# Values of a gated delta-rule layer: the four-tap convolution is moved from TensorE to VectorE

## The chip, the cores and the metric

The kernel runs on one core of one Trainium2 chip. The metric is the device time of one execution in microseconds (us). TensorE is called PE in the profile, VectorE DVE, ScalarE ACT, GpSimd POOL, and SyncE, which issues the transfers, SP.

## What is computed

The input is 8 sequences of 256 tokens with 128 channels. A feed-forward block, an attention-like block and an output projection follow one another. The change touches the first lines of the attention block:

```python
def _dwconv(x, w):                    # causal, each channel by itself, K taps
    ...
q = silu(_dwconv(hs @ Wq, conv_q))    # K = 4
k = silu(_dwconv(hs @ Wk, conv_k))
v = silu(_dwconv(hs @ Wv, conv_v))
beta = sigmoid(hs @ Wb)
o_d, _ = _delta_rule_chunkwise(bh(q), bh(k), bh(v), beta)   # chunks of 32 tokens
paths = [_dwconv(v, fir_s), _dwconv(v, fir_m), _dwconv(v, fir_l), o_d, v]
...
```

Here `hs` is the layer-normalised stream. `q` and `k` are scaled to unit length per head before the delta rule.

## The kernel before, in words

**Tiles.** The 2048 tokens are four tiles of 512 (two sequences each), with the channels on the partitions. The table `STEPS` lists steps `(kind, part, i)`, and every engine walks through that list in its order and does its own share of each step, so the list is the order of work on each engine. Part 0 is the first feed-forward, part 2 the attention, part 1 a last feed-forward. Semaphore counts come from the same list.

**Folded taps.** A convolution behind a projection is done by TensorE alone: `projections()` on VectorE multiplies a projection matrix by each tap (`taps`, one row per tap), which gives four matrices per projection in `conv_w` (12 for q, k and v, and one for beta). Each is kept as a rounded part and a rest, and so is the normalised input `xnp`; a product is three matmuls (high by high, high by low, low by high). So the step `qkv` of a tile issues 12 matmuls of 128x512 for each of q, k and v, on input shifted by one to four tokens, and 3 for beta: 39 in all (L825).

**Rings.** PSUM is eight banks: a ring `ps_a` of four that ScalarE empties (count `act_a`) and a ring `ps_d` of four that VectorE frees (count `dve_d`). `take_a(n)` and `take_d(n)` let TensorE write the n-th bank use only once use n-4 has been freed. Uses are counted in the order of `STEPS`.

**The stage around the change**, for tile t of the first two: `qkv` (t), `mean` (t+2), two `window` steps, `var` (t+2), `sumsq` (t). The steps `mean` and `var` are the layer norm of a later tile: TensorE centres (L792), ScalarE squares (L543), TensorE averages (L796), ScalarE takes a reciprocal root and squares it (L546, L549), VectorE refines the root and writes `xnp` (L985, L986, L991, L1102, L1104). The step `sumsq` sums the squares of q and k (TensorE L767), takes the root (ScalarE L621, L623) and normalises (VectorE L1155 to L1168). In `qkv` ScalarE applies Silu to q and k (L613), to the values (L608, into `vpad`), Tanh for beta (L611), and squares q and k (L616). `window` transposes pieces of `vpad` (TensorE L843, ScalarE L627). For tiles 2 and 3 there is no `mean` or `var`; the matmuls of `sumsq` 2 stand inside `qkv` 3, behind its first 12. Then `gram` 0 (TensorE L856, ScalarE L581, VectorE L1174), `lmat` (VectorE L1179), and a triangular solve on VectorE (L1069, L1072) that ends in the transposes before `yy` (L882).

## Time and profile before

| | us |
|---|---|
| median of 3 runs (lowest, highest) | 438.95 (436.8, 439.98) |
| profiled execution, its own time | 437.51 |
| its span in the trace | 435.7 |
| busy: TensorE, VectorE, ScalarE, GpSimd | 368.8, 294.9, 277.6, 42.0 |

The span is what the trace covers from the first to the last instruction; the own time is 1.8 us longer than it. Busy times overlap each other, so they don't add up to the span. The chain that ended last gives 60% of the span to TensorE, 24% to VectorE, 6% to ScalarE and 7% to stretches in which an engine waited for nothing that the profile shows ("issue").

### The profile page before, as it was taken

What the parts mean: (1) busy time and instruction counts of PE and PEld (TensorE: products, weight loads), DVE (VectorE), ACT (ScalarE), POOL (GpSimd) and SP (SyncE); (2) the same over time, 40 slices, a digit from 0 to 9 for tenths busy, and PEclk for the clock granted to TensorE, in tenths of its full rate; (3) what the DMA queues carried; (4) which work ended last, traced back from release to release, by engine and by line L of the source; (5) the groups of instructions that cost most, each with busy time, mean ns of one, the idle gap of its engine ahead of it and who ended that gap; (6) DMA issues with size and microseconds to landing.
All of it is one profiled execution on the core that took longest, in us unless ns stands there. A gap on an engine that the chain in (4) does not pass through costs nothing.

```text
span 435.7 us, 9783 instructions
## 1 busy us (share of the span) xinstructions
PE 368.8 (85%) x4132; PEld 277.2 (64%) x4132; DVE 294.9 (68%) x461; ACT 277.6 (64%) x434; POOL 42.0 (10%) x103
## 2 busy tenths in 40 slices
PE   5499999999999998799588489566599687978996
PEld 3377786678867776698477375433267464556885
DVE  1896579638307764789777968867858696478433
ACT  4788966879777786474243264515675948558963
POOL 5000000000000101000688600000000000000000
PEclk9799999999999998979955889686899898989999
DMA  7900007400000000070800000800000000001001
GB/s 267 341 3 1 3 1 214 128 2 2 1 2 0 0 2 3 3 210 16 217 5 5 2 5 2 264 5 2 0 2 3 1 2 1 2 2 50 2 2 48
DMA packets 14325, 19.75 MB, mean 45 GB/s; under 512 B 960, under 2 KB 9152, under 8 KB 14272
## 3 DMA queue, kind: packets, MB, share of 16 engines
q1 hardware_dynamic: 14128, 18.94, 14.6%
q8 instruction: 44, 0.72, 0.7%
q14 instruction: 9, 0.07, 0.1%
q10 hardware_dynamic: 144, 0.01, 0.0%
HBM read 17.91 MB, written 1.05 MB: 43 GB/s over the span
## 4 chain that ended last, share of the span: by engine, by line
PE 60%; DVE 24%; issue 7%; ACT 6%; DMA 2%; SPq 0%; DVEq 0%; ACTq 0%
PE ps_a L721 12%; PE ps_a L722 11%; PE ps_a L825 8%; PE ps_d L721 3%; PE ps_d L722 3%; PE ps_a L892 2%; PE ps_a L882 2%; DVE arena L1072 2%; DVE arena L1069 2%; PE ps_d L892 2%; PE ps_d L856 2%; PE ps_a L915 2%; DMA w_in<-in_h 2%; DVE hbuf L1114 2%; PE ps_a L913 2%
## 5 line engine op out<-in xcount | busy, mean ns | idle before, releaser
L721 PE MATMUL ps_a<-acts,w_f 128*128 128x512 f32 x256 | 103.7, 405 | 8.6 <-ACT acts L595 8.5
L722 PE MATMUL ps_a<-acts,w_f 128*128 128x512 f32 x256 | 101.6, 397 | 0.0
L721 PEld LDWEIGHTS ps_a<-acts,w_f 128*128 128x128 f32 x256 | 49.3, 192 | 22.0 <-ACT acts L595 10.2
L722 PEld LDWEIGHTS ps_a<-acts,w_f 128*128 128x128 f32 x256 | 49.2, 192 | 10.8 <-issue 0.7
L595 ACT ACTIVATE acts<-ps_a,vec 128x512 fp32r<-128x512 f32 x64 | 44.6, 697 | 0.0
L825 PE MATMUL ps_a<-xnp,conv_w 128*128 128x512 f32 x156 | 38.5, 404 | 0.0
L1138 DVE TENSOR_TENSOR acts<-gbuf,acts 128x512 fp32r<-128x512 f32 x32 | 21.6, 689 | 24.9 <-ACT acts L595 24.9
L1138 DVE TENSOR_TENSOR acts<-ghbuf,acts 128x512 fp32r<-128x512 f32 x32 | 21.2, 690 | 20.8 <-ACT acts L595 20.8
L825 PEld LDWEIGHTS ps_a<-xnp,conv_w 128*128 128x128 f32 x156 | 29.3, 188 | 8.2 <-issue 1.4
L985 DVE SCALAR_TENSOR_TENSOR arena<-ps_d,arena 128x512 f32<-128x512 f32 x16 | 11.0, 687 | 30.4 <-ACT arena L549 26.3
L592 ACT ACTIVATE gbuf<-ps_a,vec 128x512 f32<-128x512 f32 x32 | 22.3, 697 | 10.3 <-PE ps_a L722 10.1
L592 ACT ACTIVATE ghbuf<-ps_a,vec 128x512 f32<-128x512 f32 x32 | 22.4, 699 | 7.2 <-PE ps_a L722 7.1
L870 PE MATMUL ps_a<-toep,arena 96*32 96x96 f32 x512 | 23.7, 356 | 0.0
L721 PE MATMUL ps_a<-xn,w_f 128*128 128x512 f32 x32 | 15.3, 479 | 7.9 <-DVE ln L986 5.5
L870 PEld LDWEIGHTS ps_a<-toep,arena 96*32 96x32 f32 x512 | 19.3, 130 | 3.5 <-issue 1.3
L457 POOL TENSOR_TENSOR arena<-arena 128x31 f32<-128x31 f32 (+15 forms) x31 | 15.7, 505 | 46.7 <-DVE arena L1194 44.3
L904 PE MATMUL ps_d<-arena 32*32 32x64 f32 x448 | 11.7, 256 | 10.0 <-DVE arena L1222 6.6
L904 PEld LDWEIGHTS ps_d<-arena 32*32 32x32 f32 x448 | 9.0, 129 | 15.7 <-DVE arena L1222 8.3
L882 PE MATMUL ps_a<-arena 32*32 32x64 f32 x512 | 10.4, 242 | 10.1 <-DVE arena L1194 5.8
L640 ACT ACTIVATE arena<-ps_a 128x384 f32<-128x384 f32 x16 | 7.8, 490 | 16.7 <-PE ps_a L870 16.7
L1114 DVE SCALAR_TENSOR_TENSOR hbuf<-ps_d,vec,gbuf 128x512 f32<-128x512 f32 x16 | 11.6, 748 | 8.4 <-ACT gbuf L565 5.1
L459 POOL TENSOR_TENSOR arena<-arena 128x31 f32<-128x31 f32 (+15 forms) x31 | 16.7, 540 | 2.4
(211 smaller groups left out, 768.5 us busy)
## 6 DMA issues: line engine op xcount, KB each, us to landing
toep<-in_fir SPq DMA_DIRECT2D x24, 288.0 KB, 6.3
w_in<-in_h SPq DMA_DIRECT2D x4, 1024.0 KB, 8.6
g_rows<-in_gW SPq DMA_DIRECT2D x4, 640.0 KB, 6.6
w_in<-in_w SPq DMA_DIRECT2D x6, 256.0 KB, 4.4
iobuf<-in_x SPq DMA_DIRECT2D x4, 256.0 KB, 6.8
toep<-in_taps SPq DMA_DIRECT2D x1, 768.0 KB, 6.0
y<-iobuf SPq DMA_DIRECT2D x3, 256.0 KB, 2.3
toep<-in_proj SPq DMA_DIRECT2D x1, 256.0 KB, 8.6
```

The costliest lines, as they stand in the source:

```text
L459: own(e.tensor_tensor(sub, sub, prod, ALU.subtract))
L592: e.activation(gbuf[f][:, gi % 4], src[:, :], ACT.Gelu, scale=sc).then_inc(S["act_step"], 1)
L595: e.activation(acts[f][:, j % 3, 0, m], src[:, :], ACT.Gelu, scale=sc).then_inc(S["act_a"], 1)
L721: e.matmul(bank, w, hi, start=start, stop=False)
L722: return e.matmul(bank, w, lo, start=False, stop=stop)
L825: last = e.matmul(bank, conv_w[:, hw, ww], xnp[:, hx, 2 * i:2 * i + 2, o:o + L], start=n == 0, stop=n == len(todo) - 1)
L870: last = e.matmul(bank[32 * h:32 * h + 32, WIN * c4:WIN * c4 + WIN], vt[half][0:WIN, DH * h + 8 * grp + dl, :], toep[0:WIN, grp % 2, h, :, ...
L882: last = e.matmul(bank[r, 64 * n:64 * n + 64], xt[r, g, h, n], vk[r, g, h, n].rearrange("p x c -> p (x c)"), start=True, stop=True)
L892: last = e.matmul(bank[c, 64 * n:64 * n + 64], yu[r, g, h, n, o:o + DH], alt[g][r, h, n, 1:3].rearrange("p x c -> p (x c)"), start=True, s ...
L904: last = e.matmul(bank[r, 64 * b:64 * b + 64].rearrange("p (x t) -> p x t", x=2), s_sb[r, g, b], aqs[g][r, b, n], start=True, stop=True)
L1114: e.scalar_tensor_tensor(out=hbuf[f][:, m % 2], in0=ps_d[:, (dd + m) % NRING], scalar=vc("s2", m), in1=gbuf[f][:, (KT * j + m) % 4], op0=A ...
L1138: e.tensor_tensor(acts[f][:, j % 3, 1, m], gbuf[f][:, (KT * j + m) % 4], acts[f][:, j % 3, 0, m].bitcast(F32), ALU.subtract).then_inc(S["d ...
```

## The change

The values leave the step `qkv`. A new step `vproj` multiplies the normalised input by the unfolded `Wv`: three matmuls into one bank of the ring `ps_d`. VectorE then convolves from that bank into a buffer `vacc` (two of them, one per parity of the tile): one multiplication by the last tap, then three multiply-adds on shifted columns, each waiting for the one before. ScalarE's Silu reads `vacc` instead of PSUM, at the head of its share of `qkv`, and counts in `act_v`. `vproj` of tile 0 stands ahead of everything in the attention part, `vproj` of tile t+1 behind `qkv` of tile t. The folded weights shrink from 13 to 10 matrices; the four value taps reach `vec` by a second small transfer on ScalarE's queue.

```diff
-    s = []
+    s = [("vproj", 2, 0)]
     for t in range(2):
-        s += [("qkv", 2, t), ("mean", 2, t + 2), ("window", 2, 2 * t), ("window", 2, 2 * t + 1),
+        s += [("qkv", 2, t), ("vproj", 2, t + 1), ("mean", 2, t + 2), ("window", 2, 2 * t), ("window", 2, 2 * t + 1),
               ("var", 2, t + 2), ("sumsq", 2, t)]
-    s += [("qkv", 2, 2), ("window", 2, 4), ("window", 2, 5), ("sumsq", 2, 2), ("qkv", 2, 3), ("gram", 2, 0), ("lmat", 2, 0),
+    s += [("qkv", 2, 2), ("vproj", 2, 3), ("window", 2, 4), ("window", 2, 5), ("sumsq", 2, 2), ("qkv", 2, 3), ("gram", 2, 0), ("lmat", 2, 0),
...
-            e.dma_start(vec[:, 0:NVEC], d["vec"]).then_inc(S["ld_vec"], 16)
+            e.dma_start(vec[:, 0:NVEC], d["vec"][:, 0:NVEC]).then_inc(S["ld_vec"], 16)
+            e.dma_start(vc("vtap", 0, TAPS), d["vec"][:, NVEC:NVEC + TAPS]).then_inc(S["ld_vec"], 16)
...
-                    for w in range(4):
+                    e.wait_ge(S["dve_d"], D_AT[("vproj", 2, i)] + 1)
+                    e.activation(vpad[:, 2 * i:2 * i + 2, HIST:HIST + L], vacc[k2], ACT.Silu).then_inc(S["act_v"], 1)
+                    for w in range(3):
...
+                elif kind == "vproj":
+                    e.wait_ge(S["dve_xn"], VAR_AT[("var", 2, i)] + 1)
+                    bank = take_d(dd).rearrange("p (b t) -> p b t", b=2)
+                    for n, (hw, hx) in enumerate(((0, 0), (0, 1), (1, 0))):
+                        last = e.matmul(bank, conv_w[:, hw, 2 * TAPS], xnp[:, hx, 2 * i:2 * i + 2, PAD:PAD + L],
+                                        start=n == 0, stop=n == 2)
+                    last.then_inc(S["pe_d"], 1)
...
-                for w in range(3):
+                for w in range(2):
                     own(e.tensor_tensor(conv_s[:, TAPS * w:TAPS * w + TAPS],
...
-                own(e.tensor_copy(conv_s[:, 12], proj[:, 3]))
+                own(e.tensor_copy(conv_s[:, 2 * TAPS:NW], proj[:, 2:4]))
...
+                elif kind == "vproj":
+
+                    acc, z = vacc[i % 2], ps_d[:, dd % NRING].rearrange("p (b t) -> p b t", b=2)
+                    e.wait_ge(S["pe_d"], dd + 1)
+                    if i >= 2:
+                        e.wait_ge(S["act_v"], i - 1)
+                    own(e.tensor_scalar(acc, z, vc("vtap", TAPS - 1), None, ALU.mult))
+                    for back in range(1, TAPS):
+                        settle()
+                        tap = e.scalar_tensor_tensor(out=acc[:, :, back:L], in0=z[:, :, 0:L - back], scalar=vc("vtap", TAPS - 1 - back),
+                                                     in1=acc[:, :, back:L], op0=ALU.mult, op1=ALU.add)
+                        if back < TAPS - 1:
+                            own(tap)
+                        else:
+                            tap.then_inc(S["dve_d"], 1)
```

**TensorE around `sumsq` 1.** The rows show the last parts of `qkv` 1, the layer norm of tile 3, two windows (`ident,arena`), and `sumsq` 1 (`head_w`). Before:

```order
L825 MATMUL ps_a1<-xnp,conv_w 128x512 [waits act_a]
L825 MATMUL ps_a1<-xnp,conv_w 128x512 x11
L825 MATMUL ps_a2<-xnp,conv_w 128x512 [waits act_a]
L825 MATMUL ps_a2<-xnp,conv_w 128x512 x2
L792 MATMUL ps_d<-x_t,cent_w 128x512 [waits dve_d]
L843 MATMUL ps_a3<-ident,arena 96x128 [waits act_a]
L843 MATMUL ps_a3<-ident,arena 96x128 x3
L843 MATMUL ps_a0<-ident,arena 96x128 [waits act_a]
L843 MATMUL ps_a0<-ident,arena 96x128 x3
L796 MATMUL ps_d<-arena,mean_w 128x512 [waits dve_d,act_sq]
L767 MATMUL ps_d<-arena,head_w 128x512 [waits dve_d,act_ss] x2
L825 MATMUL ps_a1<-xnp,conv_w 128x512 [waits act_a,dve_xn]
```

Now:

```order
L834 MATMUL ps_a0<-xnp,conv_w 128x512 [waits act_a]
L834 MATMUL ps_a0<-xnp,conv_w 128x512 x2
L822 MATMUL ps_d<-xnp,conv_w 128x512 [waits dve_d,dve_xn]
L822 MATMUL ps_d<-xnp,conv_w 128x512 x2
L795 MATMUL ps_d<-x_t,cent_w 128x512 [waits dve_d]
L852 MATMUL ps_a1<-ident,arena 96x128 [waits act_a]
L852 MATMUL ps_a1<-ident,arena 96x128 x3
L852 MATMUL ps_a2<-ident,arena 96x128 [waits act_a]
L852 MATMUL ps_a2<-ident,arena 96x128 x3
L799 MATMUL ps_d<-arena,mean_w 128x512 [waits dve_d,act_sq]
L770 MATMUL ps_d<-arena,head_w 128x512 [waits dve_d,act_ss] x2
L834 MATMUL ps_a3<-xnp,conv_w 128x512 [waits act_a]
```

The 12 matmuls of the values (here into `ps_a1`) are gone, and three for tile 2's values stand behind the beta of tile 1. The second `head_w` matmul takes the use of `ps_d` four behind `vproj` 2 (uses 42 and 38 of the ring), so its wait for `dve_d` is now for the end of the convolution of tile 2's values; before, the use four behind belonged to the second matmul of `sumsq` 0 (its wait ended with VectorE's first two steps on it).

**VectorE between `sumsq` 0 and `var` 3.** The rows show the last normalisation of k of tile 0, kb (L1168, now L1193) and the start of the layer norm of tile 3. Before:

```order
L986 SCALAR_TENSOR_TENSOR arena<-arena 128x512
L991 SCALAR_TENSOR_TENSOR arena<-arena 128x8x32 [waits dve_step,dve_d]
L991 SCALAR_TENSOR_TENSOR arena<-arena 128x8x32
L1168 TENSOR_TENSOR arena<-arena 128x2x8x32 [waits dve_step]
L985 SCALAR_TENSOR_TENSOR arena<-ps_d,arena 128x512 [waits act_t]
L986 SCALAR_TENSOR_TENSOR arena<-ps_d,arena 128x512
L991 SCALAR_TENSOR_TENSOR arena<-arena 128x512 [waits dve_step,dve_d]
```

Now:

```order
L995 SCALAR_TENSOR_TENSOR arena<-arena 128x512
L1000 SCALAR_TENSOR_TENSOR arena<-arena 128x8x32 [waits dve_step,dve_d]
L1000 SCALAR_TENSOR_TENSOR arena<-arena 128x8x32
L1193 TENSOR_TENSOR arena<-arena 128x2x8x32 [waits dve_step]
L1167 TENSOR_SCALAR arena<-ps_d,vec 128x512 [waits act_v,pe_d]
L1170 SCALAR_TENSOR_TENSOR arena<-ps_d,vec,arena 128x2x255 [waits dve_step]
L1170 SCALAR_TENSOR_TENSOR arena<-ps_d,vec,arena 128x2x254 [waits dve_step]
L1170 SCALAR_TENSOR_TENSOR arena<-ps_d,vec,arena 128x2x253 [waits dve_step]
L994 SCALAR_TENSOR_TENSOR arena<-ps_d,arena 128x512 [waits act_t]
L995 SCALAR_TENSOR_TENSOR arena<-ps_d,arena 128x512
```

The four steps of the convolution of tile 2 stand between them.

**ScalarE at the first `qkv`.** Before:

```order
L613 ACT_TABLE_LOAD [waits pad_zero,conv_round,pe_a,act_a]
L613 ACTIVATE arena<-ps_a1 128x512 [waits dve_d]
L613 ACTIVATE arena<-ps_a2 128x512 [waits pe_a]
L608 ACTIVATE arena<-ps_a3 128x2x256 [waits pe_a]
L611 ACTIVATE arena<-ps_a0 128x512 [waits pe_a]
L616 ACTIVATE arena<-arena 128x512 [waits act_a]
```

Now:

```order
L609 ACT_TABLE_LOAD [waits pad_zero,conv_round,dve_d,act_a]
L609 ACTIVATE arena<-arena 128x2x256 [waits dve_d]
L616 ACTIVATE arena<-ps_a1 128x512 [waits pe_a]
L616 ACTIVATE arena<-ps_a2 128x512 [waits pe_a]
L614 ACTIVATE arena<-ps_a3 128x512 [waits pe_a]
L619 ACTIVATE arena<-arena 128x512 [waits act_a]
```

Silu of the values moved to the head and reads SBUF (`arena`), and it waits for VectorE's convolution.

## Rows read from the trace of the kernel before

**Rows 1.** Page, part 5: columns as busy us, mean ns, idle before.

```profile
L825 PE MATMUL ps_a<-xnp,conv_w 128*128 128x512 f32 x156 | 38.5, 404 | 0.0
L1114 DVE SCALAR_TENSOR_TENSOR hbuf<-ps_d,vec,gbuf 128x512 f32<-128x512 f32 x16 | 11.6, 748 | 8.4 <-ACT gbuf L565 5.1
```

**Rows 2.** The chain that ended last, 112 to 180: start us, us, what.

```profile
115.34 9.14 PE ps_a L825 x39
...
124.51 0.60 ACT arena L611
...
126.14 0.49 ACT arena L543
...
126.68 1.12 PE ps_d L796 x2
127.81 1.72 PE ps_d L767 x4
129.52 9.10 PE ps_a L825 x39
...
164.46 2.88 PE ps_d L856 x213
167.34 1.61 issue
168.95 0.68 PE ps_d L856 x32
...
170.07 0.42 DVE arena L1174
170.50 1.86 DVE arena L1179
```

**Rows 3.** Windows, one stretch: length, busy PE, PEld, DVE, ACT, POOL, PEclk.

```profile
124.48:129.52 5.04, 4.56 (x17) 2.33 (x17) 0.00 (x0) 4.98 (x8) 0.00 (x0) 1.00 0.02 3
```

**Rows 4.** Timeline, VectorE, 111.5 to 178: start, duration, line, [idle before].

```profile
130.39 0.69 DVE L985 SCALAR_TENSOR_TENSOR arena<-ps_d,arena 128x512 f32<-128x512 f32 x1 [14.26 <-ACT arena L549]
...
133.51 0.42 DVE L1155 TENSOR_SCALAR arena<-arena 128x512 f32<-128x512 f32 x1
...
135.18 0.68 DVE L986 SCALAR_TENSOR_TENSOR arena<-arena 128x512 f32<-128x512 f32 x1
135.89 0.76 DVE L991 SCALAR_TENSOR_TENSOR arena<-arena 128x256 f32<-128x256 f32 x2
...
138.69 0.69 DVE L1168 TENSOR_TENSOR arena<-arena 128x512 f32<-128x512 f32 x1
144.43 0.69 DVE L985 SCALAR_TENSOR_TENSOR arena<-ps_d,arena 128x512 f32<-128x512 f32 x1 [5.05 <-ACT arena L549]
```

**Rows 5.** Timeline, ScalarE, 111.5 to 178.

```profile
118.26 1.28 ACT L613 ACT_TABLE_LOAD   x1 [2.02 <-PE ps_a L825]
...
127.61 1.28 ACT L546 ACT_TABLE_LOAD   x1
...
164.99 1.14 ACT L616 ACTIVATE arena<-arena 128x512 f32<-128x512 f32 x2
```

**Rows 6.** Timeline, VectorE, 62 to 71.5, the end of `projections`.

```profile
67.29 1.89 DVE L978 TENSOR_TENSOR conv_w<-toep,conv_w 128x1664 fp32r<-128x1664 f32 x1
...
70.62 1.40 DVE L1114 SCALAR_TENSOR_TENSOR ghbuf<-ps_d,vec,ghbuf 128x512 f32<-128x512 f32 x2
```

**Rows 7.** Timeline, ScalarE, 60 to 84.

```profile
69.62 1.27 ACT L565 ACTIVATE ghbuf<-ps_a,vec 128x512 f32<-128x512 f32 x2
```

**Rows 8.** Timeline, TensorE, 353 to 387: two waits of VectorE or ScalarE.

```profile
357.21 0.50 PE L721 MATMUL ps_a<-acts,w_f 128*128 128x512 f32 x1 [1.76 <-ACT acts L595]
...
383.76 0.50 PE L721 MATMUL ps_d<-acts,w_f 128*128 128x512 f32 x1 [2.86 <-DVE arena L986]
```

**Rows 9.** Windows behind these waits: busy of each engine, then PEclk.

```profile
357.50:361.00 3.50, 3.50 (x16) 2.63 (x15) 3.43 (x6) 2.74 (x4) 0.00 (x0) 1.00 0.02 5
...
384.50:388.00 3.50, 3.49 (x10) 2.24 (x9) 3.40 (x6) 0.00 (x0) 0.00 (x0) 0.51 0.00 0
```

More of the change, by code:

```diff
@@ L19 @@
 TAPS = 4
+NW = 2 * TAPS + 2
 PAD = 4
@@ L98 @@
 STEPS = ffn_steps(0) + att_steps() + ffn_steps(1)
-RING_A = {"in": 1, "flag": 1, "gsum": 1, "up": KT, "hid1": KT, "hid2": KT, "out": 1, "qkv": 4, "window": 1, "token": 1, "fir": 1,
+RING_A = {"in": 1, "flag": 1, "gsum": 1, "up": KT, "hid1": KT, "hid2": KT, "out": 1, "qkv": 3, "window": 1, "token": 1, "fir": 1,
           "yy": 1, "bo": 1, "gate": 2, "logit": 1, "addmix": 1}
-RING_D = {"mean": 1, "var": 1, "up": KT, "down": 1, "sumsq": 2, "gram": H, "aq": 1, "rec": 1,
+RING_D = {"vproj": 1, "mean": 1, "var": 1, "up": KT, "down": 1, "sumsq": 2, "gram": H, "aq": 1, "rec": 1,
           "wo": 1}
@@ L183, in program @@
         pick = sb("pick", [128, 48])
-        vec = sb("vec", [128, 56])
+        vec = sb("vec", [128, 60])
         ct = ExitStack()
@@ L194, in program @@
         w_f = [sb("w_f0", [128, 5632], F32R, c1)]
[L195 removed]
+        conv_w = sb("conv_w", [128, 2, NW, 128], F32R, c1)
+        sb("vacc1", [128, 768], F32, c1)
         acts = [sb("acts0", [128, 3, 2, KT, TILE], F32R, c1)]
@@ L271, in program @@
         qs = at("qs", 10, TILE)
+        vacc = [at(f"vacc{k}", 2, L) for k in range(2)]
         sq_p = at("sq", 2, DH, DH)
@@ L284, in program @@
         tflat = toep[:, :, :, :, :].rearrange("p a h d x -> p (a h d x)")
-        taps = tflat[:, 0:1536]
+        taps = tflat[:, 0:1024]
         proj = tflat[:, 1536:2048].rearrange("p (i n) -> p i n", i=4)
-        conv_s = tflat[:, 2048:2048 + 13 * 128].rearrange("p (i n) -> p i n", i=13)
+        conv_s = tflat[:, 2048:2048 + NW * 128].rearrange("p (i n) -> p i n", i=NW)
         gx_s = tflat[:, 3712:3968]
@@ L340, in set_free @@
                     e.wait_ge(S["pe_a"], A_AT[user] + KT)
-        ENTRY = {("qkv", 2, 0): 2}
+        ENTRY = {("vproj", 2, 0): 2}
         def load_weights(e, stage, first, second, rest):
@@ L368, in _ @@
             e.dma_start(proj, d["proj"].rearrange("p (i n) -> p i n", i=4)).then_inc(S["ld_proj"], 16)
-            e.dma_start(taps, d["taps"].to_broadcast([128, 1536])).then_inc(S["ld_proj"], 16)
+            e.dma_start(taps, d["taps"].to_broadcast([128, 1024])).then_inc(S["ld_proj"], 16)
             e.dma_start(gx_s, d["gW1"][0:D, :]).then_inc(S["ld_proj"], 16)
@@ L444, in _ @@
             e.memset(at("tinv0", DH * DH)[:, 0:DH * DH:DH + 1], 1.0).then_inc(S["eye_done"], 1)
-            e.wait_ge(S["pe_a"], A_AT[("qkv", 2, NT - 1)] + 4)
+            e.wait_ge(S["pe_a"], A_AT[("qkv", 2, NT - 1)] + 3)
             own(e.memset(at("tinv1", DH * DH), 0.0))
@@ L607, in _ @@
                         if w == 2:
-                            e.activation(vpad[:, 2 * i:2 * i + 2, HIST:HIST + L],
-                                         src.rearrange("p (b t) -> p b t", b=2), ACT.Silu).then_inc(S["act_a"], 1)
-                        elif w == 3:
                             e.activation(qs[:, 4 + k2], src, ACT.Tanh, scale=0.5).then_inc(S["act_a"], 1)
@@ L817, in _ @@
                         e.wait_ge(S["xn_pad"], 1)
-                    e.wait_ge(S["dve_xn"], VAR_AT[("var", 2, i)] + 1)
-                    for w in range(4):
+                    for w in range(3):
                         bank = take_a(a + w)[:, :].rearrange("p (b t) -> p b t", b=2)
-                        todo = [(w * TAPS + j, 1 + j) for j in range(TAPS)] if w < 3 else [(12, PAD)]
+                        todo = [(w * TAPS + j, 1 + j) for j in range(TAPS)] if w < 2 else [(2 * TAPS + 1, PAD)]
                         todo = [(ww, o, hw, hx) for ww, o in todo for hw, hx in ((0, 0), (0, 1), (1, 0))]
@@ L837, in _ @@
                     if kind == "window" and i % 4 == 0:
-                        e.wait_ge(S["act_a"], A_AT[("qkv", 2, i // 4)] + 3)
+                        e.wait_ge(S["act_v"], i // 4 + 1)
                     bank = take_a(a)
@@ L1151, in _ @@
                                            ).then_inc(S["dve_d"], 1)
+                elif kind == "vproj":
[12 more added lines that the diff above has]
+                            tap.then_inc(S["dve_d"], 1)
                 elif kind == "sumsq":
                     k2 = i % 2
-                    e.wait_ge(S["act_a"], A_AT[("qkv", 2, i)] + 4)
+                    e.wait_ge(S["act_a"], A_AT[("qkv", 2, i)] + 3)
+                    e.wait_ge(S["act_v"], i + 1)
                     own(e.tensor_scalar(qs[:, 4 + k2], qs[:, 4 + k2], 0.5, 0.5, ALU.mult, ALU.add))
@@ L1278, in lay_out @@
            np.tile(a["L0_attn_norm_w"], H)[:, None], np.repeat(a["L0_attn_log_tau"], DH)[:, None],
-           gb2.reshape(128, 1), cols("L0_attn_gb1"), np.repeat(a["L0_attn_eps_logit"], DH, axis=0)]
-    taps = np.stack([a["L0_attn_conv_" + k].T for k in "qkv"]).reshape(1, 3 * TAPS * D)
+           gb2.reshape(128, 1), cols("L0_attn_gb1"), np.repeat(a["L0_attn_eps_logit"], DH, axis=0),
+           a["L0_attn_conv_v"]]
+    taps = np.stack([a["L0_attn_conv_" + k].T for k in "qk"]).reshape(1, 2 * TAPS * D)
     proj = [a["L0_attn_Wq"], a["L0_attn_Wk"], a["L0_attn_Wv"], np.repeat(a["L0_attn_Wb"], DH, axis=1)]
```

11 lines of the change are left out of this document (5 added, 6 removed).

## The prediction

> **What bounds the kernel now.** I read the chain of waits first: it says which engine the end waited for. From 115.3 to 164.5 us it is nearly all TensorE [rows 2]: 39 matmuls of `qkv` in 9.14 us (0.234 us each), a few short steps, the next 39. TensorE's clock is granted in full there (1.00, which is 2.4 GHz) [rows 3]. The page counts 156 such matmuls [rows 1]. In the gap between two `qkv` TensorE is busy 4.56 of 5.04 us [rows 3]: it pauses 0.48 us until ScalarE has squared tile 2's centred input (L543, done at 126.63), and the averaging matmul behind the pause takes 1.12 us where one that doesn't restart takes half of 1.72, 0.86 [rows 2]. So a pause costs 0.74 us, twice in the stage. Next I read the other engines by time. VectorE idles 14.26 us before its first work of the stage and 5.05 before the second [rows 4]: there is room, but it is not evenly spread. From 130.39 its work for one tile runs without a gap to 139.38, 9.0 us. Behind the stage the chain goes through `gram` 0, with a TensorE pause of 1.61 us, then to VectorE (L1174, L1179) and the solve [rows 2].
>
> **TensorE's part.** Each tile loses 12 matmuls and gains 3: 36 fewer in all, by 0.234 us, **-8.43 us**, all on the chain. A tile is then 30 matmuls, 7.02 us. The three matmuls of the next values (0.70 us) stand between the beta matmuls and `mean`, where TensorE used to run ahead of ScalarE: they fill the pause of 0.48. The square of L543 ends 2.15 us after the last beta matmul (126.63 less 124.48) [rows 2], and TensorE now needs 0.70 + 1.72 = 2.42 us for `vproj`, `mean` and the windows (1.72 is 4.56 less 1.12 less 1.72 [rows 2, 3]). Both pauses go: **-1.48 us**.
>
> **The convolution on VectorE.** The trace of before has no such step. The nearest rows are a multiply-add of 128x512 with one operand in PSUM and a scalar from a column of `vec`: 0.748 us (L1114) [rows 1]. A step that waits for the one before starts 0.03 us after its end (135.18 + 0.68, then 135.89) [rows 4]. So three multiply-adds and the first multiplication at the same price are 4 x 0.75 + 3 x 0.03 = 3.1 us a tile. The lower bound takes the multiplication as L1155, 0.42 us from SBUF [rows 4], and the others as 0.68: 2.6 us. The shifted, uneven columns are in no row; the nearest step that reads in another order than it writes is the transpose L1179, 1.86 us for 1024 columns [rows 2], 0.93 for 512: by it the upper bound is 4 x 0.93 + 0.09 = 3.8 us. I take 3.1, since L1114 shares the operands, the scalar and the source. The row with the fast multiplication reads SBUF. The Trainium skill says, in "VectorE: DVE Perf Modes", section "Why PSUM operands drop a tier", that a PSUM operand of fp32 runs at the plain rate: by that rule the multiplication is not at 0.42, and the sum stays with 3.1; by the row it would be 0.3 us a tile less.
>
> For tiles 0 and 1 the cost is nil: VectorE is idle until 130.4, and the convolution of tile 0 (116.1 to 119.2, behind the last L1149) and that of tile 1 (about 123.1 to 126.2) lie in that gap [rows 4]. ScalarE waits for the first at its head; then its table load (1.28) and Silu (0.60) [rows 2, 5] end at 121.1, and q's Silu at 121.7, when k's matmuls end (115.34 + 27 x 0.234 = 121.66). Nothing is late, by a hair; if that cover is gone, each 0.1 us more goes into the chain.
>
> **A new wait.** Tile 2's convolution is not free. I follow the stage in the times of before. `qkv` 0 ends at 115.34 + 7.02 = 122.4, windows at 124.8, `var` 2 at 125.65, `sumsq` 0 at 127.4, then `qkv` 1 with `vproj` 2 to 134.4. The averaging matmul of `var` 2 lets ScalarE and then VectorE start: before, VectorE began 2.58 us after `sumsq` 0's predecessor ended (130.39 less 127.81), and ScalarE's table load stood behind two window copies which now end at 125.6. So VectorE starts at 125.65 + 2.78 = 128.4 (2.78 is 130.39 less the table load's 127.61 [rows 4, 5]) and ends tile 0's normalisation at 137.4. Only then comes tile 2's convolution, in line ahead of `var` 3: 137.4 to 140.45. TensorE meanwhile does `mean` 3, the windows and `var` 3 to 137.0 and the first matmul of `sumsq` 1 to 137.85. The second needs the PSUM bank that the convolution reads, and waits: 2.6 us, and 0.25 to restart, **+2.85 us**. Queued behind it on TensorE is `qkv` 2; on ScalarE the root of k's sums waits for it, on VectorE tile 1's normalisation, which starts behind `var` 3 anyway. By the bounds of the convolution (2.6 and 3.8) the wait is 2.4 to 3.6.
>
> Tile 3's convolution follows tile 1's normalisation: 149.4 to 152.5, against TensorE's `qkv` 3, which ScalarE must not yet have begun. Tile 2's sums then reach VectorE at 154.5 and free their banks by 157, ahead of the last part of `gram` 0 (about 159.7). ScalarE ends its squares of tile 3 about 3 us behind `qkv` 3 instead of 1.65 (164.99 + 1.14 less 164.46 [rows 2, 5]), but its last copy of `gram` 0 waits for a TensorE that pauses 1.61 us and ends 5.17 us behind `qkv` 3 [rows 2]: hidden. If that pause shrank, ScalarE would be next, 0.6 us or so behind. `qkv` 3 thus ends at 164.46 - 8.43 - 1.48 + 2.85 = 157.4.
>
> **Small parts.** `projections` on VectorE handles 10 matrices instead of 13: L978 falls from 1.89 to 1.45 us, with L969 and L975 about 1.2 in all; it stands right ahead of the first L1114 of tile 2's feed-forward (70.62), but that also needs ScalarE's first L565, done at about 70.3 [rows 6, 7]. So **-0.3 us** (0 to -0.35). The second small transfer on ScalarE's queue falls into its idle start; the taps' transfer is a third shorter and hidden; both at nothing. Behind `gram` 0 every step hangs on its predecessors, not on a fixed time, so the shift is handed on.
>
> **The sum:** -8.43 - 1.48 + 2.85 - 0.3 = **-7.4 us** from the profiled execution's 437.5, giving 430.1. That execution lies 1.4 below the median of the runs, 438.95; from the median it is **431.5 us**.
>
> **Rivals.** (a) *The clock falls at the new wait.* A wait of 1.76 us in dense matmuls left the granted clock at 1.00; one of 2.86 was followed by 3.5 us at 0.51 (1.2 GHz) [rows 8, 9]. The new one, 2.6, lies between. Half of 3.5 us is lost, +1.75: 433.3. For it: 2.6 is nearer to 2.86. Against: TensorE works off a full stretch before and after. (b) *The wait is shorter or absent*, because VectorE starts earlier or the steps are cheaper: without it 431.5 - 2.85 = 428.7. Against it: VectorE's 9.0 us are fixed and its start hangs on ScalarE. (c) *Part is given back later*: behind the stage TensorE pauses "for nothing the profile shows" (1.61 us at 167.3) [rows 2], and 7% of the chain is such pauses; if an earlier TensorE is held by them 2 to 6 us longer, 433.5 to 437.5. Against it: the pauses stand behind work of VectorE and small matmuls which all move together. (d) *Slower than before: VectorE becomes the bound.* If a convolution costs c instead of 3.1, tile 0's delays ScalarE and tile 2's the bank, so the end is later by about 2(c - 3.1) - 0.3. It decides from 2(c - 3.1) = 7.7, c = 6.9 us, 1.7 us a step; at 2 us a step the time is 431.5 + 9.5 = 441. Against it: every row of such a step is under 0.8 us. For it only that shifted columns of a PSUM bank are in no row.
>
> **Chances.** Forecast as it stands (430 to 433) 0.45; (a) 0.25; (b) 0.08; (c) 0.18, of which a third still beats 434.6; (d) 0.04. A difference under about 1% (4.4 us) can't be told from none in this kernel, whose three runs spread over 3.2 us. So faster 0.45 + 0.25 + 0.08 + 0.06 = 0.84; the rest of (c) is the same, 0.12; slower 0.04. The range takes in (b)'s near end, the bounds of the convolution, (a) and half of (c): 429 to 435.5.
>
> **What would show it.** The 120 matmuls of `qkv` and `vproj` at 0.234 us; no wait of L799 for L547; the first L770 pair of tile 1 with a wait of about 2.6 us for VectorE L1170, and the clock behind it; L1170 at 0.75 us and back to back with L1193; the `qkv` of tile 3 ending 7 us earlier; the rest of the trace shifted whole. The prediction is wrong if L1170 is over 1 us, if the clock falls in several places, or if the distance from `gram` 0 to the end grows.

## The result and the profile after

The changed kernel takes 431.73 us (median of 4 runs, 430.13 to 432.02) against 437.96 us for the kernel before (4 runs, 436.8 to 439.98): a ratio of 0.984 [0.981, 0.986]. The forecast was 431.5 us. Six more runs of the same kernel, further below, gave 430.47; the kernel before, run 11 to 27 times beside the experiments, had medians of 437.8 to 438.3. The profiled execution took 430.13 us, with a span of 428.4 us; forecast from that of the kernel before, it was 430.1.

The page of the kernel after, parts 1 and 5:

```profile
PE 359.4 (84%) x4096; PEld 269.8 (63%) x4096; DVE 305.1 (71%) x476; ACT 276.7 (65%) x434; POOL 42.0 (10%) x103
...
L834 PE MATMUL ps_a<-xnp,conv_w 128*128 128x512 f32 x108 | 27.3, 407 | 0.0
```

TensorE lost 9.4 us of busy time (a matmul at half clock counts as busy for longer, and in a later trace of the same kernel TensorE was busy 362.7 us, so not all of the 9.4 is work removed); VectorE gained 10.2. The chain that ended last, from the first value projection to the second matmul pair of `sumsq` 1 and on to the solve (start us, us, what):

```profile
114.77 0.69 PE ps_d L822 x3
115.46 6.33 PE ps_a L834 x27
...
121.82 0.60 ACT arena L614
122.42 0.96 ACT arena L619 x2
...
125.01 1.28 ACT L550
...
127.68 0.69 DVE arena L994
...
136.57 0.76 DVE arena L1167
...
137.36 0.76 DVE arena L1170
...
138.14 0.76 DVE arena L1170
...
138.92 0.76 DVE arena L1170
139.68 0.14 issue
139.81 1.10 PE ps_d L770 x2
140.91 6.33 PE ps_a L834 x27
...
159.53 0.28 ACT arena L585
...
159.83 1.42 DVE arena L1199 x4
161.25 1.88 DVE arena L1204
```

Before, this chain was TensorE's almost alone [rows 2]. Now the 27 matmuls of q, k and beta take 6.33 us (0.234 each), and between two such runs the chain goes through ScalarE's root and VectorE's normalisation and convolution: TensorE waits for the bank that tile 2's convolution reads. TensorE's timeline shows that wait and what came of the pauses behind the stage (start, duration, line, [idle before <- what ended it]):

```profile
139.81 1.10 PE L770 MATMUL ps_d<-arena,head_w 128*128 128x512 f32 x2 [2.32 <-DVE arena L1170]
...
156.75 3.40 PE L865 MATMUL ps_d<-arena 32*32 32x64 f32 x256
...
161.64 0.64 PE L852 MATMUL ps_a<-ident,arena 128*96 128x128 f32 x4 [0.91 <-ACT arena L630]
...
200.42 2.44 PE L891 MATMUL ps_a<-arena 32*32 32x64 f32 x160 [1.73 <-DVE arena L1219]
207.31 2.78 PE L891 MATMUL ps_a<-arena 32*32 32x64 f32 x96 [4.46 <-issue]
...
215.11 1.55 PE L901 MATMUL ps_d<-arena 32*32 32x64 f32 x54 [1.88 <-issue]
```

Where the time went, by the starts in the two timelines: the stage, from its first matmul to the first of `gram` 0, shrank from 49.21 us (115.18 to 164.39) to 42.14 (114.61 to 156.75), by 7.07. `gram` 0 lost its pause of 1.61 us [rows 2], and the transpose L1204 (L1179 before) starts 9.25 us earlier than before (161.25 against 170.50 [rows 2]). The lead is 9.45 us at `yy` (200.42 against 209.87) and 6.90 at `rec` (226.17 against 233.07). Of these 2.55 us given back, 1.89 are TensorE's pauses for nothing that the profile shows ("issue"), which grew from 6.94 to 8.83 us there. The rest is in the matmuls of `yy`, 5.22 us instead of 4.50: the last 96 ran at half clock here, before only the last four. At the end the lead is 7.3 us: from the first matmul of `gram` 0 to the end it is 271.65 us here and was 271.31 before.

### The profile page after: what moved, and what is told of

The parts are those of the page before. It is cut to its first block, busy times and chain, and to the rows that moved or that the text cites. A ratio compares the mean times of both kernels' runs of the same rounds, so it can differ in the third digit from the quotient of the medians.

```text
span 428.4 us, 9734 instructions
## 1 busy us (share of the span) xinstructions
PE 359.4 (84%) x4096; PEld 269.8 (63%) x4096; DVE 305.1 (71%) x476; ACT 276.7 (65%) x434; POOL 42.0 (10%) x103
## 4 chain that ended last, share of the span: by engine, by line
PE 55%; DVE 27%; ACT 7%; issue 7%; DMA 2%; SPq 0%; DVEq 0%; ACTq 0%
PE ps_a L724 12%; PE ps_a L725 12%; PE ps_a L834 4%; PE ps_d L724 3%; PE ps_d L725 3%; PE ps_a L891 3%; PE ps_a L901 3%; DVE arena L1078 2%; DVE arena L1081 2%; PE ps_d L901 2%; PE ps_a L924 2%; DMA w_in<-in_h 2%; DVE hbuf L1123 2%; PE ps_a L922 2%; PE ps_d L913 2%
## 5 line engine op out<-in xcount | busy, mean ns | idle before, releaser
L724 PEld LDWEIGHTS ps_a<-acts,w_f 128*128 128x128 f32 x256 | 49.3, 192 | 22.0 <-ACT acts L599 10.2
L596 ACT ACTIVATE gbuf<-ps_a,vec 128x512 f32<-128x512 f32 x32 | 22.3, 697 | 10.2 <-PE ps_a L725 10.1
L834 PE MATMUL ps_a<-xnp,conv_w 128*128 128x512 f32 x108 | 27.3, 407 | 0.0
L834 PEld LDWEIGHTS ps_a<-xnp,conv_w 128*128 128x128 f32 x108 | 20.2, 188 | 6.0 <-issue 1.4
L460 POOL TENSOR_TENSOR arena<-arena 128x31 f32<-128x31 f32 (+15 forms) x31 | 15.6, 503 | 44.8 <-DVE arena L1219 42.5
L891 PEld LDWEIGHTS ps_a<-arena 32*32 32x32 f32 x512 | 10.4, 135 | 11.4 <-DVE arena L1219 6.7
L1123 DVE SCALAR_TENSOR_TENSOR hbuf<-ps_d,vec,gbuf 128x512 f32<-128x512 f32 x16 | 11.6, 748 | 8.3 <-ACT gbuf L569 4.1
```

What stands on the lines that cost most here:

```text
L460: own(e.tensor_tensor(prod, lmat[1][:, j + 1:DH, j:j + 1].to_broadcast(shape), tinv[1][:, j:j + 1, 0:j + 1].to_broadcast(shape), ALU.mult))
L596: e.activation(gbuf[f][:, gi % 4], src[:, :], ACT.Gelu, scale=sc).then_inc(S["act_step"], 1)
L724: e.matmul(bank, w, hi, start=start, stop=False)
L834: last = e.matmul(bank, conv_w[:, hw, ww], xnp[:, hx, 2 * i:2 * i + 2, o:o + L], start=n == 0, stop=n == len(todo) - 1)
L891: last = e.matmul(bank[r, 64 * n:64 * n + 64], xt[r, g, h, n], vk[r, g, h, n].rearrange("p x c -> p (x c)"), start=True, stop=True)
L1123: e.scalar_tensor_tensor(out=hbuf[f][:, m % 2], in0=ps_d[:, (dd + m) % NRING], scalar=vc("s2", m), in1=gbuf[f][:, (KT * j + m) % 4], op0=A ...
```

## The experiments

### One cost more or less: tile 2's convolution

**two_taps_less**: two of tile 2's three multiply-adds left out, so the values of that tile are not the reference's.

```diff
-                    for back in range(1, TAPS):
+                    for back in ((TAPS - 1,) if i == 2 else range(1, TAPS)):
```

> The changed kernel, but VectorE leaves out two of the three shifted multiply-adds of tile 2's values (its output is therefore not the reference's). Theory 1 (the wait of the second sumsq matmul of tile 1 is on the path and lasts as long as VectorE's convolution): the convolution of tile 2 ends 1.56 us sooner, TensorE's wait falls from 2.3 to about 0.8 us, everything up to gram 0 comes 1.56 us sooner, and the time is 1.5 us under the changed kernel's (430.2 against 431.7). Theory 2 (the stage is bound elsewhere, by ScalarE's or TensorE's own work): the wait shrinks in the trace, and the start of gram 0 and the time move by less than 0.4 us.

Measured: 428.52 us (426.6 to 430.08), 0.980 [0.975, 0.984] of before; profiled 427.57. The wait of L770 shrank from 2.32 to 0.76 us, by the two steps of 0.78, and `gram` 0 starts 1.44 us earlier (155.31). By theory 1 the time was to fall by 1.5 us. The rest of the gain, some 1.1 us in the two traces, stands from `yy` on, where the pauses are shorter (3.77 us instead of 4.46 in `yy`); it isn't the wait's. The wait stands on the chain with its whole length.

**twice_tile2**: tile 2's convolution is done twice over; the result is unchanged.

```diff
-                    own(e.tensor_scalar(acc, z, vc("vtap", TAPS - 1), None, ALU.mult))
+                    for rep in range(2 if i == 2 else 1):
+                      ...
+                      own(e.tensor_scalar(acc, z, vc("vtap", TAPS - 1), None, ALU.mult))
```

> The changed kernel, with VectorE's convolution of tile 2's values done twice (same result, 3.1 us more on VectorE). Theory 1 (the bank wait is on the path one for one): TensorE's wait grows from 2.3 to 5.4 us; gram 0 starts 3.1 us later. After so long a wait I expect TensorE's granted clock at half for some 3.4 us, another 1.7 us: in all 3 to 5 us over the changed kernel (435 to 436.5). Theory 2 (VectorE has room, since the next layer norm waits for ScalarE anyway): under 1.5 us more.

Measured: 435.78 us (435.59 to 436.8), 0.996 [0.994, 0.998]; profiled 436.8. TensorE's timeline, and windows over the wait and behind it (length, busy PE, PEld, DVE, ACT, POOL, PEclk, DMA share, GB/s):

```profile
142.45 2.04 PE L770 MATMUL ps_d<-arena,head_w 128*128 128x512 f32 x2 [5.46 <-DVE arena L1173]
```

```profile
137.00:142.40 5.40, 0.00 (x0) 0.00 (x0) 5.19 (x8) 2.75 (x5) 0.00 (x0) 0.90 0.00 0
142.40:147.40 5.00, 4.95 (x10) 3.27 (x11) 4.86 (x9) 2.80 (x4) 1.33 (x2) 0.50 0.00 0
147.40:152.00 4.60, 4.60 (x20) 3.68 (x19) 3.70 (x8) 1.19 (x3) 0.00 (x0) 0.92 0.01 2
```

The wait grew by 3.14 us, and behind it the granted clock was 0.50 for 5 us (1.2 GHz), so that what followed cost about 2.6 us more (`qkv` 2 starts 1.06 us behind the end of the wait instead of 0.53, and its 27 matmuls take 8.99 us instead of 6.89): the stage took 47.91 us instead of 42.14. So a second convolution of 3.1 us took most of the gain of the change, as theory 1 has it.

**twice_tile0**: the same for tile 0 (`i == 0`), whose convolution was to be hidden "by a hair".

> The changed kernel, with VectorE's convolution of tile 0's values done twice (same result, 3.1 us more). The prediction called tile 0's cover exact to a tenth of a us: ScalarE's Silu for q and k and Tanh then end about 3 us later, and with them the square in front of var 2, VectorE's start and the rest: gram 0 and the time 2.5 to 3.1 us later than the changed kernel (434.2 to 434.8). Rival: ScalarE catches up, since TensorE's qkv 0 runs on until 121.8 us: under 1 us later.

Measured: 433.71 us (432.95 to 438.92, 10 runs), 0.991 [0.989, 0.994], about 2 us over the changed kernel.

```profile
126.66 1.12 PE L799 MATMUL ps_d<-arena,mean_w 128*128 128x512 f32 x2 [1.85 <-ACT arena L547]
...
142.40 1.10 PE L770 MATMUL ps_d<-arena,head_w 128*128 128x512 f32 x2 [0.61 <-DVE arena L1173]
```

The pause before `var` 2 is back, longer than the 0.48 us it had before the change, and TensorE idles another 0.62 us shortly ahead of it, until ScalarE's Silu of the values is done. Behind the 1.85 the clock fell too, here in the windows of that stretch:

```profile
121.00:128.00 7.00, 4.52 (x19) 2.57 (x18) 3.59 (x5) 6.27 (x11) 0.00 (x0) 0.98 0.00 0
128.00:134.00 6.00, 6.00 (x17) 3.50 (x16) 3.61 (x7) 5.87 (x8) 0.00 (x0) 0.74 0.01 3
```

The stage took 44.96 us, 2.8 longer than in the changed kernel. VectorE's normalisation started 2.8 us later in it; TensorE, slowed by the clock, came to `sumsq` 1 another 1.7 us later than that, and the wait there shrank by as much, from 2.32 to 0.61. So the lost clock cost nothing here. The cover was nearly as thin as forecast: of 3.1 us more, 2.8 arrived. The runs lie a little below the 434.2 to 434.8 us expected.

### The order of the steps, with and without the change

**early_norm**: the layer norm of tile 2 stands ahead of `qkv` 0, so that VectorE normalises before it convolves tile 2.

```diff
-    s = [("vproj", 2, 0)]
-    for t in range(2):
-        s += [("qkv", 2, t), ("vproj", 2, t + 1), ("mean", 2, t + 2), ...
+    s = [("vproj", 2, 0), ("mean", 2, 2), ("var", 2, 2)]
+    s += [("qkv", 2, 0), ("vproj", 2, 1), ("mean", 2, 3), ("window", 2, 0), ("window", 2, 1), ("var", 2, 3), ("sumsq", 2, 0)]
+    s += [("qkv", 2, 1), ("vproj", 2, 2), ("window", 2, 2), ("window", 2, 3), ("sumsq", 2, 1)]
```

> The changed kernel with the layer norm of tiles 2 and 3 one tile earlier in the order: mean 2 and var 2 right behind vproj 0, mean 3 and var 3 in tile 0's share. VectorE does var 2 in its idle time during qkv 0. Theory 1 (VectorE's queue in front of tile 2's convolution makes the bank wait): the 2.3 us wait of the second sumsq matmul of tile 1 goes, against a new pause of about 0.6 us of TensorE in front of var 2; gram 0 comes 2.2 us sooner, the time is near 429.5 against the changed kernel's 431.7. Theory 2 (the wait is worth nothing, another engine ends the stage): gram 0 and the time stay within 0.5 us, or get later by the 0.6 us pause.

**early_norm_before**: the same order in the kernel before.

> The kernel before with the same earlier layer norm of tiles 2 and 3. There VectorE has idle time and no bank wait; one of the two pauses of 0.48 us goes (that of tile 1), and a pause of about 1.3 us comes in front of var 2, which has no vproj ahead of it. By theory 1 the order is worth nothing here: 0 to 1 us slower than the kernel before. If it gains 2 us here too, the gain of the order has nothing to do with VectorE's convolution.

Measured: early_norm 427.49 us (427.13 to 429.07, 5 runs), 0.975 [0.973, 0.978]; early_norm_before 438.7 us (436.68 to 439.88), 1.001 [0.999, 1.003]. TensorE's timeline in early_norm has no wait at `sumsq` 1, here the last row:

```profile
136.44 0.87 PE L821 MATMUL ps_d<-xnp,conv_w 128*128 128x512 f32 x3
137.14 1.03 PE L851 MATMUL ps_a<-ident,arena 128*96 128x128 f32 x8
138.01 1.88 PE L769 MATMUL ps_d<-arena,head_w 128*128 128x512 f32 x4
```

A pause of 0.8 us before `var` 2 takes its place. The stage takes 40.44 us instead of 42.14, as the wait less the pause says. The order by itself is worth nothing, since before the change there was no such wait; it removes what the change brought. The medians lie 4.2 us apart (3.0 from the later set of the changed kernel, below), more than the 1.7 of the traces; what the rest is, the traces don't show, and the profiled execution of early_norm, 429.07 us, was the slowest of its five. All five are faster than the ten executions of the changed kernel.

### The pauses behind the stage

TensorE's pauses of 1 to 5 us for nothing that the profile shows moved between the two kernels. In both, the last transfers of the `toep` tables run beside `yy`. First, two runs hold the last eight back until `yy` is over.

**late_fir_after**, and **late_fir_before** with the same edit in the kernel before:

```diff
                 e.wait_ge(S["pe_a"], A_AT[("fir", 2, last_use)] + 1)
+                if grp == 0:
+                    e.wait_ge(S["pe_a"], A_AT[("yy", 2, 3)] + 1)
                 load_toep(e, grp)
```

> The changed kernel, with the last eight transfers of FIR weights (2.3 MB) held until the step yy of the first half is done, so that they don't run beside yy. Theory 3 (TensorE's pauses without a cause in the profile, 4.46 us in yy and more behind it, come from the transfers running beside it, which slow the supply of TensorE's instructions): the pause in yy falls below 1.5 us, and the time by 2 to 4 us, to about 429. Theory 4 (the pauses come from the stream of many small instructions itself): pauses and time stay within 1 us. If the weights land too late for the last FIR steps, those wait instead, which the trace would show as a DMA wait of TensorE.

> The kernel before, with the same eight transfers held until yy of the first half is done. Theory 3: its pauses of 1.13 and 3.24 us in yy go too, so it gains 2 to 4 us, somewhat less than the changed kernel does, whose pauses there are longer. Theory 4: no change, within 1 us.

Measured: late_fir_after 430.81 us (430.08 to 434.47), 0.987 [0.982, 0.992]; late_fir_before 438.59 us (435.6 to 440.99), 1.001 [0.998, 1.005]. TensorE's timeline in late_fir_after:

```profile
199.98 5.40 PE L893 MATMUL ps_a<-arena 32*32 32x64 f32 x256 [1.51 <-DVE arena L1221]
206.10 0.64 PE L903 MATMUL ps_d<-arena 32*32 32x64 f32 x31 [0.72 <-ACT arena L649]
207.01 1.78 PE L903 MATMUL ps_d<-arena 32*32 32x64 f32 x127 [0.27 <-issue]
212.86 1.55 PE L903 MATMUL ps_d<-arena 32*32 32x64 f32 x54 [4.07 <-issue]
```

The pause of 4.46 us in `yy` is gone, and one of 4.07 stands where the transfers now run. It moves with them. `rec` came 1.7 us earlier (224.46), and the time stayed, which theory 3 had not foreseen: the next `yy` took 6.63 us instead of 5.83, over 250 to 254 us the granted clock was 0.66 against 1.00, and by 274 us the two traces are level. In late_fir_before the pauses inside `yy` fell from 1.13 and 3.24 us to 0.94 in all and `rec` came 2.3 us earlier (230.78 against 233.07), but the 2 to 4 us of theory 3 did not come: then VectorE waited for GpSimd's half of the solve, which ended only 0.4 us earlier than in the kernel before (246.9 against 247.3):

```profile
246.92 1.93 DVE L1196 STREAM_TRANSPOSE arena<-arena 128x1024 f32<-128x1024 f32 x1 [0.34 <-POOL vec L462]
```

The lengths between pauses hint at what TensorE waits for. From 160 of the 256 matmuls of `yy` on they are 96 + 31, 127, and so on (counting across steps), here and in the changed kernel. The profile also has a queue for instructions. The DMA view, 202 to 208 us of the changed kernel, across its pause in `yy` (queue: packets, MB, share of 16 engines):

```profile
q1 hardware_dynamic: 300, 0.77, 45.7%
q8 instruction: 1, 0.02, 1.3%
```

One read of the instruction queue, about 16 KB (over 196 to 230 us it is seven reads, 0.11 MB). In windows of 0.1 us, it stands at 204.7, and the matmuls go on at 207.31. The profile doesn't say which engine the queue feeds; that it is TensorE is inferred from how reads and pauses go together. The read at 209.1 has no pause behind it, since TensorE is waiting for ScalarE there; the later reads and the ends of the pauses behind them go in pairs: 212.6 and 215.11, 216.3 and 218.92, 220.6 and 223.01, 224.2 and 226.17. In late_fir_after the first of them stands at 201.1, before the transfers begin, and `yy` has no pause; the one at 210.3, beside the transfers, is followed by the restart at 212.86. The Trainium skill says, in "Advanced Engine Details and Errata", section "ISA Cache", that an engine's instructions are cached in lines of 16 KB, 256 instructions each; it gives 32 KB in all, 128 KB for TensorE, and beside it "Only 2 cache lines!". By this rule a line holds 128 matmuls with their weight loads, which is an estimate from the page; the trace agrees, with pieces of 125 to 127. How many lines TensorE has, no run here shows. The prediction did not draw on it.

If so, it is the place in the instruction stream, not the step, that fixes where a pause can stand. The change took 36 matmuls and 36 weight loads out ahead of it. The first cut of `yy` does stand 35 matmuls later than before (behind 160 instead of 125), and the one of `gram` 0 went by 36, from behind its 224th matmul to behind the 4th of the two windows that follow its 256. There the changed kernel idles 0.91 us up to 161.64, behind a read of the instruction queue at 159.2. The profile puts this idle time down to L630, but by the ring the bank that these matmuls write was free once the Silu of q was done, by 157.5. So the pause of `gram` 0 was not lost; it moved behind the results that VectorE waits for.

**shifted_stream**: the changed kernel, with 18 fp32 matmuls of one column (two matmuls and two weight loads each) ahead of TensorE's first step.

```diff
             e.wait_ge(S["consts"], 1)
+            for n in range(18):
+                e.matmul(ps_a[0][:, 0:1], mean_w[:, :], mean_w[:, 0:1], start=True, stop=True)
```

> The changed kernel with 18 one-column fp32 matmuls (36 weight loads and 36 matmul instructions) at TensorE's idle start, where they cost nothing: every later TensorE instruction stands as far down the stream as in the kernel before. Theory 4b (pauses without a cause depend on where in TensorE's instruction stream a run of small matmuls falls): the pause of 1.6 us in gram 0 comes back, the one of 4.46 us in yy becomes 1.1 and 3.2 as before, and the time moves by 0 to 2 us. Theory 3b (they depend on when the runs and the transfers fall in time): the trace looks like the changed kernel's, no pause in gram 0.

Measured: 436.71 us (435.14 to 437.92, 10 runs), 0.996 [0.994, 0.998]. Most of the loss was the experiment's own: the added matmuls ran 7.84 us ahead of the first layer norm, and the stage began 5.95 us later. The clock behind the wait at `sumsq` 1 fell as well, of which more below. But the pauses came back to the places of the kernel before, in `gram` 0 and at the end of `yy` nearly to its sizes (1.86 and 2.97 us; before 1.61 and 3.24), as TensorE's timeline shows:

```profile
169.11 0.65 PE L867 MATMUL ps_d<-arena 32*32 32x64 f32 x32 [1.86 <-issue]
...
210.24 1.98 PE L893 MATMUL ps_a<-arena 32*32 32x64 f32 x125 [1.35 <-DVE arena L1221]
212.62 2.10 PE L893 MATMUL ps_a<-arena 32*32 32x64 f32 x127 [0.40 <-issue]
```

**shifted_hidden** repeats it with 36 matmuls on 16-bit operands, which took 1.12 us.

```diff
+            half = mean_w[:, :].bitcast(mybir.dt.bfloat16)
+            for n in range(36):
+                e.matmul(ps_a[0][:, 0:1], half[:, 0:128], half[:, 0:1], start=True, stop=True)
```

> The changed kernel with 36 matmuls of one column each (16-bit operands, so one matmul and one weight load apiece) issued before TensorE's first transposition, where the chain runs through the load of the weights and TensorE has several microseconds to spare (it idles 5.44 us before its first projection). They move every later TensorE instruction as far down the stream as it stands in the kernel before. Seen so far in shifted_stream: 5.95 us of its loss stand ahead of the first value projection (its 18 fp32 matmuls ran 7.84 us and pushed the normalisation back), and from there to the end it takes 315.0 us against 313.6. Theory A, pauses stand where 16 KB blocks of TensorE's instructions end (the profile's instruction queue reads one such block every 3.6 us or more, and the pieces of small matmuls between pauses are 125 to 128 long, two instructions each): a pause of 1.6 to 1.9 us in gram 0, 0.4 and 3.0 us in yy (pieces x125, x127), 0.5, 1.2 and 1.1 us behind, the first value projection within 0.3 us of 114.8, and an own time 1 to 2 us over the changed kernel's 430.1, thus 431 to 432.5. Theory B, the pauses belong to the earlier arrival itself: no pause in gram 0, 4.5 us in yy, own time 430.1. Theory C, the extra matmuls cost what they did in shifted_stream wherever they hide: 435 or more.

Measured: 430.54 us (429.29 to 432.69 and one of 435.82, 6 runs), 0.981 [0.978, 0.984]: no different from the changed kernel by the medians, where theory A expected 1 to 2 us more. In its trace (span 430.9) `gram` 0 is cut behind 224 matmuls again, with a pause of 1.36 us, and `yy` behind 252, with 3.70. So the place in the stream decides where a pause can be, as theory A has it; but moving it costs nothing that these runs tell: from `gram` 0 to the end it is 271.58 us, against 271.65 in the changed kernel. The matmuls were not wholly hidden either: the stage began at 115.57 us instead of 114.61. And this trace held something else: the clock.

```profile
140.79 1.96 PE L770 MATMUL ps_d<-arena,head_w 128*128 128x512 f32 x2 [2.32 <-DVE arena L1173]
141.76 8.03 PE L837 MATMUL ps_a<-xnp,conv_w 128*128 128x512 f32 x27
```

```profile
139.79:140.79 1.00, 0.00 (x1) 0.03 (x1) 0.96 (x3) 0.97 (x3) 0.00 (x0) 1.00 0.00 0
140.79:141.79 1.00, 1.00 (x3) 0.48 (x3) 1.00 (x2) 0.51 (x1) 0.00 (x0) 0.54 0.00 0
141.79:142.79 1.00, 1.00 (x3) 0.48 (x2) 0.93 (x3) 0.00 (x1) 0.00 (x0) 0.50 0.00 0
```

The wait is the same 2.32 us, but the clock behind it fell to 0.50, and the stage took 43.75 us instead of 42.14. In the changed kernel the same microseconds read 1.00:

```profile
138.80:139.80 1.00, 0.00 (x0) 0.02 (x1) 0.96 (x3) 0.97 (x3) 0.00 (x0) 1.00 0.00 0
139.80:140.80 1.00, 0.99 (x3) 0.52 (x4) 1.00 (x2) 0.53 (x1) 0.00 (x0) 1.00 0.00 0
```

**paced_after** and **paced_early** (on early_norm): each of the last eight transfers waits for the one before, so that an instruction read has less data ahead of it. Not shown of the edit: the first transfer of the last group of four waits for the group before it, too.

```diff
+                if paced and h:
+                    e.wait_ge(S[f"ld_t{grp % 2}"], 16 * (2 * H + h))
                 e.dma_start(toep[0:WIN, grp % 2, h], rows).then_inc(S[f"ld_t{grp % 2}"], 16)
```

> The changed kernel, with each of the last eight 288 KB transfers into toep issued only when the one before it has landed, so that an instruction block read meanwhile stands behind little data on the 16 DMA engines. Theory A, the yy pause of 4.46 us is one 16 KB instruction block that waits behind the queued transfers: the pause falls to some 1 to 1.5 us, the 1.88 behind it to about 1.1, rec starts near 222.5 instead of 226.2, and the own time falls 3 to 3.5 us to about 427 (the paced transfers last to about 222, just ahead of the first matmul that reads them, once rec begins; if they are slower than 2.9 us each, that matmul waits for them and gives the gain back). Theory B, the pause has to do with how many bytes move in all and not with how they are queued: no change, 430. Theory C, the pause is only handed on to the next one, as when the transfers were held back until the end of yy: within 1 us of 430.

> The kernel with the third normalisation ahead of the first query and key projections (early_norm) and the paced toep transfers together. Theory A: the two gains stand at different places (the wait at sumsq 1 and the pause in yy, here 5.05 us), so they add: about 424, 3 us or so under early_norm's 427.5. Theory B: as early_norm, 427.5. The rival that the solve on GpSimd becomes the bound: it ended 4 us ahead of VectorE's last combination in the changed kernel, so a gain over 4 us is cut off there.

Measured: paced_after 429.79 us (426.72 to 431.93, 6 runs), 0.979 [0.975, 0.983]; paced_early 427.06 us (425.81 to 430.32, 6 runs), 0.975 [0.971, 0.979]. In paced_after's timeline:

```profile
206.88 1.54 PE L895 MATMUL ps_a<-arena 32*32 32x64 f32 x96 [1.67 <-issue]
...
210.87 2.32 PE L905 MATMUL ps_d<-arena 32*32 32x64 f32 x127 [1.09 <-issue]
215.35 1.55 PE L905 MATMUL ps_d<-arena 32*32 32x64 f32 x54 [2.16 <-issue]
```

The pause of 4.46 us fell to 1.67, near the 1 to 1.5 expected (on early_norm from 5.05 to 1.30), but those behind it didn't shrink (1.09, 2.16, 1.47, 1.00, 1.10): from `yy` to `rec` 24.71 us against 25.75. With early_norm it was 22.97 against 25.67, and 1.6 us of that were given back behind `rec`. So theory A is right about the pause: the data queued ahead of the instruction read make it long. It is wrong about the time: 427 and 424 us were expected, and neither median can be told from that of the same kernel with its transfers unpaced, which is what theory C and theory B said. In paced_after's trace the clock fell again at the wait of 2.33 us.

**after_again**: the changed kernel, unedited.

> The changed kernel once more, unedited, for its spread. In the traces so far the same wait of 2.32 us at sumsq 1 left the granted clock at 1.00 in two kernels (the changed one, late_fir_after) and was followed by about 3 us at 0.50 in three (shifted_stream, shifted_hidden, paced_after), where qkv 2 starts 0.44 us later behind the wait and takes 8.03 us instead of 6.89: 1.58 us in all, with gram 0 at 43.7 us behind the first value projection instead of 42.1. Theory A, the wait lies at the edge and the same program falls on either side: executions from 430 to 432.5, median 431 to 432, so most of them over the profiled 430.13 and the distance to gram 0 in this trace either 42.1 or 43.7. Theory B, the clock falls only where a kernel's code differs: this one never loses it, and its median lies within 0.5 us of 430.1 or its spread has another cause; the distance is 42.1.

Measured: 430.47 us (429.57 to 432.53, 6 runs), 0.984 [0.981, 0.987]. In its trace the wait is 2.32 us, the clock stayed at 1.00 and the stage took 42.15 us; the pause in `yy` was 3.01 us. The ten runs of the two sets lie from 429.57 to 432.53 with no gap between groups. So for this wait theory A isn't shown: over six traces with it unchanged, the clock fell in three and held in three, the changed kernel's own two among the latter. But at another wait the two traces of this one program do part. In after_again `yy` starts behind a wait of 1.48 us and runs its first 160 matmuls at half clock; in the first trace it starts behind a longer one, 1.73 us, and the clock held (timeline of after_again, its window 200 to 202 us, and the same window of the first trace):

```profile
199.93 4.06 PE L891 MATMUL ps_a<-arena 32*32 32x64 f32 x160 [1.48 <-DVE arena L1219]
```

```profile
200.00:202.00 2.00, 2.00 (x84) 2.00 (x88) 2.00 (x2) 0.19 (x1) 1.55 (x6) 0.52 1.04 301
```

```profile
200.00:202.00 2.00, 1.58 (x112) 1.58 (x116) 1.97 (x2) 0.42 (x1) 1.15 (x5) 1.00 1.04 298
```

This cost nothing: the 160 matmuls took 4.06 us instead of 2.44, the pause behind them 3.01 instead of 4.46, and the next block's matmuls started at 207.00 against 207.31. A pause is what is left until the block is there, so its length alone says little.

## Why the prediction was right

**The time: nearer than the forecast could know.** The change in the profiled executions was forecast as -7.4 us and measured as -7.38, but other pairs give less and more: -6.2 by the medians of the first sets, -7.75 by those of the last. And the 431.5 started from a median of three runs, 438.95, where later sets of the same kernel gave 437.8 to 438.3. To hit 431.73 within 0.3 us was luck; to lie in the range was not.

**TensorE's part: right.** 120 matmuls at 0.234 us, and no wait for the square of L547 is left in the stage. The sum of the stage was -8.43 - 1.48 + 2.85 = -7.06; measured -7.07.

**The convolution: right, at the value taken.** The multiplication took 0.76 us, the three multiply-adds 0.76 each with 0.02 between them, 3.1 in all. The row of 0.42 from SBUF was the wrong neighbour; the shifted columns cost nothing over L1114's 0.748 [rows 1]. That the first one is hidden by a hair held too: ScalarE's Tanh starts 0.03 us behind `qkv` 0's end, and by twice_tile0 the cover was some 0.3 us.

**The new wait: right in place and cause, a little shorter.** 2.32 us instead of 2.6, and with the restart (1.10 against 0.86) 2.56 instead of 2.85. VectorE started at 127.68 instead of 128.4. Two_taps_less and twice_tile2 moved it one for one.

**The small part: right in size by luck.** The stage began 0.57 us earlier than before, by its row in the chain, against -0.3. But ScalarE's L569, which doesn't depend on `projections`, was itself 0.42 us earlier (69.20 against 69.62 [rows 7]), since TensorE's first step, which waits for the first load of the input, began at 4.80 us against 5.22. The first L1123 gained 0.53 (70.09 against 70.62 [rows 6]), so about 0.1 is left for `projections`.

**Rival (a): real, and at the price given.** Behind 2.32 us the clock held in three traces and fell in three, for 1.6 us against the 1.75 forecast; behind 5.46 it fell; behind 0.76 and 0.61 it held; in twice_tile0 it fell behind 1.85 (with 0.62 idle shortly ahead), a length like that of the wait of 1.76 that had left it alone [rows 8, 9]; and at the start of `yy` the same program lost it behind 1.48 and kept it behind 1.73. So neither the length of the wait nor the kernel settles it; what does stays open. So the weight of a quarter was, if anything, low; the range took it in.

**"Behind gram 0 the shift is handed on": right in the sum, wrong step by step and in its reason.** From `gram` 0 to the end of the trace it is 271.65 us instead of 271.31, so all but 0.3 us of the shift arrived. The steps between did not move together. The pause in `gram` 0, which was to hide ScalarE, moved 36 matmuls on and out of VectorE's way (-1.61), and as the prediction had it for that case, ScalarE came next: the chain reaches VectorE through L585. The stretch from `yy` to `rec` then took 2.55 us back, of which 1.89 are pauses, rival (c)'s mechanism at the low end of its 2 to 6, and the rest goes with the clock, which fell inside `yy` here. The reason given against (c), that the pauses stand behind work which moves together, was wrong: they hang on where the instruction stream is cut into blocks and on what the DMA engines carry when the next block is read, and the change moved both. That gains and losses cancelled was luck as far as the prediction goes, since it had neither. But the sum is steadier than its parts: over the traces of all fourteen kernels and repeats the way from `gram` 0 to the end is 270.5 to 272.9 us, and 271.4 and 271.6 in shifted_stream and shifted_hidden, which have the pause in `gram` 0 again. What evens it out stays open.

**Rival (d): excluded** by the 0.76 us of each step. Of its point the runs say that twice_tile2, with 3.1 us more in one tile, lost 5.8 us in the stage, more than the one-for-one delay of the rival because the clock fell as well, so the point would come somewhat earlier than 6.9 us (an estimate from these two numbers; no run went there).
